# Taylor-attention sandwich, 1 core: the rest features in tiles of 64 rows and 32 columns, split over two PSUM banks

## The chip, the core and the metric

One core of one Trainium2 chip. The metric is the device time of one execution in microseconds (us), as the median of several runs. TensorE (PE), VectorE (DVE), ScalarE (ACT) and GpSimd (POOL) each work off a queue of their own, in order, and wait for each other on semaphores; the DMA queues are fed by SyncE (SP) and by ACT.

## What is computed

The input is 16 sequences of 512 rows of 256 numbers, float32. Cut to what matters:

```python
x = x + layernorm(attention(layernorm(x)))
x = x + layernorm(ffn(layernorm(x)))

# attention: 16 heads of 16, rotary q and k, no softmax but its Taylor form
t = 1.0 + qk + 0.5 * qk * qk
attn = t / jnp.sum(t, axis=-1, keepdims=True)
wv = einsum('bhkq,bhqd->bhkd', attn, v);  return wv @ w_o

# ffn: rows and weights rounded to an FP6 grid in blocks of 32, then one product
out = xd @ wd.T + bias
```

Because 1 + s + s*s/2 is a polynomial in products of q and k, the kernel never forms the 512 x 512 scores. It expands each head's key into features (products of pairs of its 16 numbers, squares, the numbers themselves, a one), sums features times values over the 512 rows of a sequence, and multiplies the features of the other side with these sums.

## The kernel before

The work is cut into 64 tiles of 128 rows, four to a sequence. Every engine's program is a loop over steps, `step(n)`, in which each stage is called for the tile `n` minus its lag. The table `LAG` gives the lags, `FIRST` and `FINAL` shift the first 12 and the last 16 tiles, and the order of calls inside `step` is the order on that engine (PE at lines 822 to 846). So an engine's order is written out by hand and nothing is scheduled at run time: an engine that waits holds up all that stands behind it.

One tile passes PE in these stages, here with their lines:

- `turn_z` (672): two 128x128 transposes into `ps_tr`. ACT reads them into `hT` (991), splits off the high part `hT_h` (1001), POOL the low part `hT_l` (1472).
- `project_kq` (591, 592, 594): six products of 512 columns into `ps_qk`; DVE reads that bank twice for the rotation (1270, 1278). `project_v`: six of 256 columns into `ps_tr`.
- `turn_q` (658): four transposes into `ps_tr`, read by ACT (1022). The bank `ps_tr` has four users a tile, `turn_z`, `turn_q`, `project_v`, `turn_ffn_input`, and each waits until the one before was read.
- `sum_features` (796): 16 products of 32 output rows and 161 columns into `ps_mt`, four at a time side by side in the array (tiles of 128 rows and 32 columns).
- `select_0` to `select_4` (635): each one product of 512 columns with a 0/1 matrix from the constant `selection`. ACT squares each result into a slice of `feat` (944, 946). The first four slices are one head each with 128 features; the fifth, `feat[:, p2, HQ]`, holds for four heads together the remaining 32 features of each, in rows 32h to 32h+31.
- `attend` (687, 690): for each of four heads 32 output rows and 512 columns in `ps_o`. The first product takes the head's 128 features with weights `main`. The second takes the fifth slice with weights `rm`, a 128x128 block of which only the 32x32 block of the own head is not zero. ACT copies the result into `osb` with a bias (1032), `copy_quad`.
- `turn_quads` (724) and `turn_attention` (715) in `ps_o`; `project_out` in `ps_w`; `turn_ffn_input` in `ps_tr`; `ffn` (767, 591, 592, 594) in `ps_w` too, except for the last eight tiles, where it is in `ps_qk`.

After `ffn` comes one chain across four engines: ACT sums squares (`square_f`, 1067), POOL adds a floor and takes the power -1/2 (1488, 1492), DVE scales and adds (`add_ffn`, 1388), SP stores. `project_out` has the same chain (1048, 1488, 1492, 1355).

Once a sequence, after its fourth tile, ACT copies the sums (956), PE turns them (`turn_sums`, 805), ACT copies `main` (966), PE forms the matrix of the rest (`rest_matrix`, 814, 818) and ACT copies it to `rm` (`copy_rest`, 973, four instructions).

## Time and profile before

| | us |
|---|---|
| median of 3 runs | 675.56 (674.57 to 675.61) |
| the profiled execution | 673.7 |
| its span | 671.8 |
| PE busy | 660.0, 98% |
| ACT busy | 558.0, 83% |
| DVE busy | 562.8, 84% |
| POOL busy | 335.2, 50% |

The span runs from the first to the last instruction of the profiled execution; 1.9 us lie around it. PE instructions are pipelined and the ends of their rows are modelled, so they overlap: how long a group really holds PE is read from the start of one row to the start of the next. In the middle of the kernel every tile is alike, so one tile's rows stand for all.

### The profile page before, as it was taken

What the parts mean: (1) busy time and instruction counts of PE and PEld (TensorE: products, weight loads), DVE (VectorE), ACT (ScalarE), POOL (GpSimd) and SP (SyncE); (2) the same over time, 40 slices, a digit from 0 to 9 for tenths busy, and PEclk for the clock granted to TensorE, in tenths of its full rate; (3) what the DMA queues carried; (4) which work ended last, traced back from release to release, by engine and by line L of the source; (5) the groups of instructions that cost most, each with busy time, mean ns of one, the idle gap of its engine ahead of it and who ended that gap; (6) DMA issues with size and microseconds to landing.
All of it is one profiled execution on the core that took longest, in us unless ns stands there. A gap on an engine that the chain in (4) does not pass through costs nothing.

```text
span 671.8 us, 20456 instructions
## 1 busy us (share of the span) xinstructions
PE 660.0 (98%) x6772; PEld 505.7 (75%) x6772; DVE 562.8 (84%) x1460; ACT 558.0 (83%) x1551; POOL 335.2 (50%) x723
## 2 busy tenths in 40 slices
PE   7889999999999999999999999999999999999998
PEld 6766677777777777877777787777778777777578
DVE  5998889888988888898888889888888988986675
ACT  4578999798898979888897988889798888989864
POOL 3654435545554554555455455545544554643354
PEclk8999999999999999999999999999999999999999
DMA  7101100202011010201101020111102001010101
GB/s 236 33 3 32 34 1 3 80 17 81 9 49 48 30 60 18 79 11 48 50 32 58 17 81 9 49 48 37 55 17 80 11 18 49 9 50 23 51 33 40
DMA packets 28165, 28.35 MB, mean 42 GB/s; under 512 B 1824, under 2 KB 27936, under 8 KB 28064
## 3 DMA queue, kind: packets, MB, share of 16 engines
q1 hardware_dynamic: 27248, 26.26, 12.2%
q8 instruction: 58, 0.95, 0.6%
q10 hardware_dynamic: 816, 0.79, 0.4%
q14 instruction: 43, 0.35, 0.2%
HBM read 18.65 MB, written 8.39 MB: 40 GB/s over the span
## 4 chain that ended last, share of the span: by engine, by line
PE 94%; DVE 2%; ACT 2%; issue 1%; POOL 1%; DVEq 0%; POOLq 0%; ACTq 0%
PE ps_f L635 11%; PE ps_mt L796 10%; PE ps_o L687 9%; PE ps_o L690 8%; PE ps_qk L591 5%; PE ps_qk L594 5%; PE ps_qk L592 4%; PE ps_w L591 4%; PE ps_w L592 4%; PE ps_w L594 4%; PE ps_tr L658 4%; PE ps_tr L591 4%; PE ps_o L724 4%; PE ps_tr L594 2%; PE ps_tr L592 2%; PE ps_tr L672 2%
## 5 line engine op out<-in xcount | busy, mean ns | idle before, releaser
L944 ACT ACTIVATE feat<-ps_f 128x512 f32<-128x512 f32 x256 | 153.1, 601 | 1.8 <-PE ps_f L635 1.1
L635 PE MATMUL ps_f<-qT,selr 128*128 128x512 f32 x320 | 136.1, 428 | 0.7 <-ACT feat L944 0.5
L527 DVE TENSOR_TENSOR kf<-kf 128x1024 f32<-128x1024 f32 (+1 forms) x128 | 135.7, 1095 | 0.2
L1488 POOL TENSOR_TENSOR ve_y<-var_y,epst 128x1 f32<-128x1 f32 x64 | 24.4, 382 | 167.0 <-ACT squares_y L1048 167.0
L796 PEld LDWEIGHTS ps_mt<-kf,vp 128*32 128x32 f32 x2048 | 65.5, 110 | 38.6 <-issue 35.5
L796 PE MATMUL ps_mt<-kf,vp 128*32 128x161 f32 x2048 | 82.2, 301 | 0.1
L991 ACT ACTIVATE hT<-ps_tr,small,lnwx 128x128 f32<-128x128 f32 x128 | 51.6, 454 | 24.5 <-PE ps_tr L672 23.7
L687 PE MATMUL ps_o<-feat,main 128*32 128x512 f32 x512 | 68.2, 603 | 0.0
L690 PE MATMUL ps_o<-feat,rm 128*32 128x512 f32 x512 | 67.0, 592 | 0.0
L635 PEld LDWEIGHTS ps_f<-qT,selr 128*128 128x128 f32 x320 | 60.3, 189 | 8.7 <-issue 4.7
L1488 POOL TENSOR_TENSOR ve_f<-var_f,epst 128x1 f32<-128x1 f32 x64 | 14.5, 227 | 103.6 <-ACT squares_f L1067 103.6
L1007 ACT ACTIVATE vp<-ps_tr 128x256 f32<-128x256 f32 x64 | 24.6, 384 | 46.2 <-PE ps_tr L594 44.3
L527 POOL TENSOR_TENSOR kf<-kf 128x256 f32<-128x256 f32 x64 | 49.0, 765 | 18.3 <-DVE kf L1294 18.3
L1472 POOL TENSOR_TENSOR hT_l<-hT,hT_h 128x256 fp32r<-128x256 f32 x64 | 47.1, 736 | 18.6 <-ACT hT_h L1001 18.6
L591 PE MATMUL ps_qk<-wkqv_h,hT_l 128*128 128x512 f32 x128 | 51.3, 401 | 0.0
L1477 POOL TENSOR_TENSOR qsp<-kf,qsp 128x256 fp32r<-128x256 f32 x64 | 47.0, 735 | 8.2 <-ACT qsp L1038 5.2
L592 PE MATMUL ps_qk<-wkqv_l,hT_h 128*128 128x512 f32 x128 | 50.7, 396 | 0.0
L1032 ACT ACTIVATE osb<-ps_o,cb 128x512 f32<-128x512 f32 x64 | 44.9, 701 | 2.3 <-PE ps_o L690 2.2
L946 ACT ACTIVATE feat<-ps_f,small 128x512 f32<-128x512 f32 x64 | 46.0, 719 | 0.7 <-PE ps_f L635 0.3
L1287 DVE TENSOR_TENSOR kf<-t 128x512 f32<-128x512 f32 x64 | 44.5, 696 | 1.6
L690 PEld LDWEIGHTS ps_o<-feat,rm 128*32 128x32 f32 x512 | 17.4, 110 | 37.5 <-issue 37.5
L1388 DVE SCALAR_TENSOR_TENSOR fin<-ps_w,rs_f,xs 128x256 f32<-128x256 f32 x56 | 27.0, 482 | 22.1 <-POOL rs_f L1492 22.1
(194 smaller groups left out, 1989.9 us busy)
## 6 DMA issues: line engine op xcount, KB each, us to landing
xc<-L_attn_x SPq DMA_DIRECT2D x16, 512.0 KB, 4.0
result<-fin SPq DMA_DIRECT2D x64, 128.0 KB, 1.7
xa<-L_attn_x SPq DMA_DIRECT2D x15, 512.0 KB, 4.0
wkqv<-L_attn_w_kv ACTq DMA_DIRECT2D x2, 256.0 KB, 4.8
xa<-L_attn_x SPq DMA_DIRECT2D x1, 384.0 KB, 6.3
csel<-selection SPq DMA_DIRECT2D x1, 320.0 KB, 6.7
wkqv<-L_attn_w_q ACTq DMA_DIRECT2D x1, 256.0 KB, 4.4
wf<-L_ffn_weight SPq DMA_DIRECT2D x1, 256.0 KB, 6.1
```

Of the source, the lines that this page charges most:

```text
L527: return eng.tensor_tensor(dims(row, F_MAIN, [[FW, heads], [HD, NR], [1, HD]]), dims(row, F_LIN, [[FW, heads], [0, NR], [1, HD]]), dims(ro ...
L591: pe.matmul(out_, xl(c), wh(c), start=c == 0 and not bias, stop=False)
L592: pe.matmul(out_, xh(c), wl(c), start=False, stop=False)
L594: mm = pe.matmul(out_, xh(c), wh(c), start=False, stop=c == CH - 1)
L635: pe.matmul(ps_f[i % 2][:, :], selr[:, i], qT[:, par, quad], start=True, stop=True).then_inc(sel_done, 1)
L687: pe.matmul(ps_o[VW * h:VW * (h + 1), :], main[:, par, quad, VW * h:VW * (h + 1)], feat[:, p2, h], start=True, stop=False, skip_group_chec ...
L690: mm = pe.matmul(ps_o[VW * h:VW * (h + 1), :], rm[:, par, quad, VW * h:VW * (h + 1)], feat[:, p2, HQ], start=False, stop=True, skip_group_ ...
L796: mm = pe.matmul(ps_mt[qd // 2][VW * h:VW * (h + 1), (qd % 2) * NF:(qd % 2 + 1) * NF], vp[:, s2, qd * HQ + h], kf[:, s2, qd * HQ + h, 0:NF ...
L944: act.activation(feat[:, p2, i], ps_f[i % 2][:, :], ACT.Square).then_inc(squared, 1)
L991: ins = act.activation(hT[:, c], ps_tr[:, c * P:(c + 1) * P], ACT.Identity, bias=lnb[:, c:c + 1], scale=lnwx[:, c:c + 1])
L1472: pool.tensor_tensor(hT_l[:, p2], hT[:], hT_h[:, p2].bitcast(F32), ALU.subtract).then_inc(hT_low, 1)
L1477: pool.tensor_tensor(dims(qsp[:, p2], HQ * HD, [[2 * HQ * HD, NQ], [HD, HQ], [1, HD]]), dims(kf[:, p2, 0, 0:1], F_Q, [[HQ * FW, NQ], [FW, ...
```

## The change

- The fifth slice. Its 32 features a head are in 32 of 128 rows, so 64 rows hold two heads. `select_4` becomes two products of 256 columns: the first 256 columns with the selection as before, the last 256 with a second selection matrix in which the heads are moved by two places (rows of heads 0, 1 and of heads 2, 3 change places).
- `attend` writes columns 0 to 255 to `ps_o` and columns 256 to 511 to `ps_w` (`quad_bank`). The products with `main` become eight of 256 columns in place of four of 512. The products with the rest become eight of 64 rows and 32 columns, 256 columns long. For heads 0 and 1 the first part takes array rows 0 to 63 and the second part rows 64 to 127, for heads 2 and 3 the other way round.
- The second part needs the rest weights in the other half of the rows: `copy_rest` on ACT waits for its own copy and issues two DMAs from `rm` to a second buffer `rm_moved`, once a sequence.
- `copy_quad` becomes two ACT instructions of 256 columns.
- `ps_w` now holds half of `attend`, so `ffn` goes to `ps_qk` for all tiles. `project_kq` now waits for `fin_ready`, the end of the chain behind `ffn`; `ffn` waits for both readings of keys and queries; `attend` waits for `xs_ready`, and `project_out` for `o_copied`.
- The selection constant grows from five to six blocks and is loaded into `osb` (alias `csel`).
- The tables `LAG`, `FIRST`, `FINAL` and the order of calls in every `step` are new.

```diff
-    "fill_a": 0, "warm_up": -19, "turn_ffn_input": 15, "rest_matrix": 4, "fill_b": 2, "drain_a": 16, "attend": 8,
+    "warm_up": -20, "drain_b": 16, "turn_z": 0, "rest_matrix": 3, "project_kq": 1, "select_0": 7,
...
+                sel[:, h, i, HQ + 1, ((h + 2) % HQ * 2 + kind) * HD + i] = 1.0
...
+        quad_bank = [ps_o, ps_w]
...
-                pe.matmul(ps_f[i % 2][:, :], selr[:, i], qT[:, par, quad], start=True, stop=True).then_inc(sel_done, 1)
+                if i < HQ:
+                    pe.matmul(ps_f[i % 2][:, :], selr[:, i], qT[:, par, quad], start=True, stop=True).then_inc(sel_done, 1)
+                else:
+                    for part in range(2):
+                        mm = pe.matmul(ps_f[0][:, part * TH:(part + 1) * TH], selr[:, HQ + part], qT[:, par, quad, part * TH:(part + 1) * TH],
+                                       start=True, stop=True)
+                    mm.then_inc(sel_done, 1)
...
+                wait(pe, xs_ready, issued["project_out"])
+                wait(pe, wdt_copied, CH * issued["turn_ffn_weight"])
                 pe.wait_ge(rm_copied, t.seq + 1)
+                pe.wait_ge(rest_moved, 32 * (t.seq + 1))
                 pe.wait_ge(squared, CHUNKS * (n + 1))
-                for h in range(HQ):
-                    pe.matmul(ps_o[VW * h:VW * (h + 1), :], main[:, par, quad, VW * h:VW * (h + 1)], feat[:, p2, h],
-                              start=True, stop=False, skip_group_check=True)
-                for h in range(HQ):
-                    mm = pe.matmul(ps_o[VW * h:VW * (h + 1), :], rm[:, par, quad, VW * h:VW * (h + 1)], feat[:, p2, HQ],
-                                   start=False, stop=True, skip_group_check=True)
+                for part in range(2):
+                    for h in range(HQ):
+                        pe.matmul(quad_bank[part][VW * h:VW * (h + 1), 0:TH], main[:, par, quad, VW * h:VW * (h + 1)],
+                                  feat[:, p2, h, part * TH:(part + 1) * TH], start=True, stop=False, skip_group_check=True)
+                for part in range(2):
+                    for h in range(HQ):
+                        half = (h // 2 + part) % 2
+                        rows = slice(64 * half, 64 * half + 64)
+                        weights = (rm, rm_moved)[part]
+                        mm = pe.matmul(quad_bank[part][VW * h:VW * (h + 1), 0:TH], weights[rows, par, quad, VW * h:VW * (h + 1)],
+                                       feat[rows, p2, HQ, part * TH:(part + 1) * TH], start=False, stop=True, skip_group_check=True)
...
             def project_kq(t):
...
                 wait(pe, qk_read, 2 * (t.n - 1))
+                wait(pe, fin_ready, issued["ffn"])
...
             def ffn(t):
...
+                wait(pe, qk_read, 2 * issued["project_kq"])
+                wait(pe, fin_ready, issued["ffn"])
...
             def copy_rest(t):
...
                 ins.then_inc(rm_copied, 1)
+                act.wait_ge(rm_copied, t.seq + 1)
+                for half in range(2):
+                    act.dma_start(rm_moved[64 * half:64 * half + 64, mpar], rm[64 - 64 * half:128 - 64 * half, mpar]).then_inc(rest_moved, 16)
...
             def copy_quad(t):
...
-                act.activation(osb[:, par, quad], ps_o[:, :], ACT.Identity, bias=cb[:, par, quad:quad + 1]).then_inc(o_copied, 1)
+                for part in range(2):
+                    ins = act.activation(osb[:, par, quad, part * TH:(part + 1) * TH], quad_bank[part][:, 0:TH], ACT.Identity,
+                                         bias=cb[:, par, quad:quad + 1])
+                ins.then_inc(o_copied, 1)
...
```

Where the rows move. First PE around `attend`, in a tile in the middle, before (a name in brackets is a semaphore that the instruction waits for, x3 a count):

```order
L645 MATMUL ps_tr<-small,xd 128x128
L687 MATMUL ps_o<-feat,main 32x512 [waits rm_copied,aT_low,squared,norm_ready,o_copied]
L687 MATMUL ps_o<-feat,main 32x512 x3
L690 MATMUL ps_o<-feat,rm 32x512 x4
L796 MATMUL ps_mt0<-kf,vp 32x161 [waits sq_ready,feat_ready2,v_copied,feat_ready1,feat_ready0]
L796 MATMUL ps_mt0<-kf,vp 32x161 x7
L796 MATMUL ps_mt1<-kf,vp 32x161 x8
L591 MATMUL ps_tr<-wkqv_h,hT_l 128x256 [waits xdT_low,qT_copied,v_copied,hT_copied,hT_low]
```

And the same place on PE after the change:

```order
L618 MATMUL ps_f1<-qT,selr 128x512 [waits squared]
L790 MATMUL ps_mt0<-kf,vp 32x161 [waits sq_ready,feat_ready2,v_copied,feat_ready1,feat_ready0]
L790 MATMUL ps_mt0<-kf,vp 32x161 x7
L790 MATMUL ps_mt1<-kf,vp 32x161 x8
L680 MATMUL ps_o<-feat,main 32x256 [waits wdt_copied,rm_copied,xs_ready,rest_moved,aT_low,squared,norm_ready,o_copied]
L680 MATMUL ps_o<-feat,main 32x256 x3
L680 MATMUL ps_w<-feat,main 32x256 x4
L688 MATMUL ps_o<-feat,rm 32x256 x4
L688 MATMUL ps_w<-feat,rm_moved 32x256 x4
L572 MATMUL ps_tr<-wkqv_h,hT_l 128x256 [waits xdT_low,qT_copied,v_copied,hT_copied,hT_low]
```

`sum_features` has moved ahead of `attend`, and between the 32-column products of 128 rows and the full-width products of `project_v` there are now products of 64 rows.

Second, PE around `project_kq` before, behind the last selection of a tile (`ps_f`):

```order
L635 MATMUL ps_f0<-qT,selr 128x512 [waits squared]
L591 MATMUL ps_qk<-wkqv_h,hT_l 128x512 [waits qk_read,hT_low]
L592 MATMUL ps_qk<-wkqv_l,hT_h 128x512
L591 MATMUL ps_qk<-wkqv_h,hT_l 128x512
L592 MATMUL ps_qk<-wkqv_l,hT_h 128x512
L594 MATMUL ps_qk<-wkqv_h,hT_h 128x512 x2
L724 MATMUL ps_o<-small,osb 128x128 [waits norm_ready,aT_low,o_copied]
L724 MATMUL ps_o<-small,osb 128x128 x3
L672 MATMUL ps_tr<-small,z 128x128 [waits xdT_low,qT_copied,v_copied,hT_copied,z_ready]
L672 MATMUL ps_tr<-small,z 128x128
```

And after:

```order
L622 MATMUL ps_f0<-qT,selr 128x256 [waits squared]
L622 MATMUL ps_f0<-qT,selr 128x256
L722 MATMUL ps_o<-small,osb 128x128 [waits norm_ready,aT_low,o_copied]
L722 MATMUL ps_o<-small,osb 128x128 x3
L661 MATMUL ps_tr<-small,z 128x128 [waits xdT_low,qT_copied,v_copied,hT_copied,z_ready]
L661 MATMUL ps_tr<-small,z 128x128
L572 MATMUL ps_qk<-wkqv_h,hT_l 128x512 [waits fin_ready,qk_read,hT_low]
L573 MATMUL ps_qk<-wkqv_l,hT_h 128x512
L572 MATMUL ps_qk<-wkqv_h,hT_l 128x512
L573 MATMUL ps_qk<-wkqv_l,hT_h 128x512
L575 MATMUL ps_qk<-wkqv_h,hT_h 128x512 x2
```

`project_kq` has moved behind `turn_quads` and `turn_z` and waits for `fin_ready`. From the end of `ffn` to it PE now passes `turn_attention`, `select_3`, `turn_q`, `project_out`, the two halves of `select_4`, `turn_quads` and `turn_z`.

Third, ACT once a sequence, where it copies the rest matrix, before:

```order
L991 ACTIVATE hT<-ps_tr,small,lnwx 128x128 [waits hT_low,zT_done]
L991 ACTIVATE hT<-ps_tr,small,lnwx 128x128
L944 ACTIVATE feat<-ps_f0 128x512 [waits quad_done,sel_done]
L1061 ACTIVATE squares_s,var_s<-c3 128x256 [waits rstd_s,centred]
L1048 ACTIVATE squares_y,var_y<-ps_w 128x256 [waits rstd_y,wo_done]
L1014 ACTIVATE xdT_h<-ps_tr 128x256 [waits ffn_done,xdT_done]
L1001 ACTIVATE hT_h<-hT 128x256 [waits v_done,qk_done,hT_copied]
L973 ACTIVATE rm<-ps_mt0 32x4x32 [waits ps_done]
L973 ACTIVATE rm<-ps_mt0 32x4x32 x3
```

And after:

```order
L1043 ACTIVATE kf<-kf 128x16x16 [waits rope_ready]
L988 ACTIVATE hT<-ps_tr,small,lnwx 128x128 [waits hT_low,zT_done]
L988 ACTIVATE hT<-ps_tr,small,lnwx 128x128
L967 ACTIVATE rm<-ps_mt0 32x4x32 [waits ps_done]
L967 ACTIVATE rm<-ps_mt0 32x4x32 x3
L971 DMA rm_moved<-rm 64x512 [waits rm_copied]
L971 DMA rm_moved<-rm 64x512
L998 ACTIVATE hT_h<-hT 128x256 [waits v_done,qk_done,hT_copied]
L1061 ACTIVATE squares_s,var_s<-c3 128x256 [waits rstd_s,centred]
```

The copy of the rest matrix, with a wait for its own end and two DMA issues behind it, now stands ahead of `hT_h` and of all that follows in that step.

## Rows read from the trace of the kernel before

**Rows 1.** The page: span, busy time, chain by engine, DVE's products of features.
```profile
span 671.8 us, 20456 instructions
PE 660.0 (98%) x6772; PEld 505.7 (75%) x6772; DVE 562.8 (84%) x1460; ACT 558.0 (83%) x1551; POOL 335.2 (50%) x723
...
PE 94%; DVE 2%; ACT 2%; issue 1%; POOL 1%; DVEq 0%; POOLq 0%; ACTq 0%
...
L527 DVE TENSOR_TENSOR kf<-kf 128x1024 f32<-128x1024 f32 (+1 forms) x128 | 135.7, 1095 | 0.2
```

**Rows 2.** Busy time by stretch: us, each engine, PE clock, DMA share, GB/s.
```profile
400.00:500.00 100.00, 100.00 (x1027) 77.26 (x1027) 84.64 (x225) 86.42 (x243) 51.43 (x113) 1.00 0.12 38
640.00:671.80 31.80, 29.81 (x234) 26.04 (x234) 21.75 (x72) 16.49 (x61) 15.48 (x42) 1.00 0.12 38
```

**Rows 3.** Timeline of PE: start, length, engine, line, tiles, form, count.
```profile
305.95 0.48 PE L818 MATMUL ps_mt<-small,rest 128*32 128x32 f32 x32
306.38 1.06 PE L687 MATMUL ps_o<-feat,main 128*32 128x512 f32 x8
...
313.77 0.60 PE L724 MATMUL ps_o<-small,osb 128*128 128x128 f32 x4
314.21 0.38 PE L672 MATMUL ps_tr<-small,z 128*128 128x128 f32 x2
...
315.61 0.38 PE L645 MATMUL ps_tr<-small,xd 128*128 128x128 f32 x2
315.92 1.06 PE L687 MATMUL ps_o<-feat,main 128*32 128x512 f32 x8
316.81 1.04 PE L690 MATMUL ps_o<-feat,rm 128*32 128x512 f32 x8
317.67 1.28 PE L796 MATMUL ps_mt<-kf,vp 128*32 128x161 f32 x32
318.87 0.39 PE L591 MATMUL ps_tr<-wkqv_h,hT_l 128*128 128x256 f32 x1
319.10 0.28 PE L592 MATMUL ps_tr<-wkqv_l,hT_h 128*128 128x256 f32 x1
319.22 0.28 PE L591 MATMUL ps_tr<-wkqv_h,hT_l 128*128 128x256 f32 x1
...
325.41 1.06 PE L687 MATMUL ps_o<-feat,main 128*32 128x512 f32 x8
...
345.53 1.06 PE L687 MATMUL ps_o<-feat,main 128*32 128x512 f32 x7
```

**Rows 4.** Timeline of PE and its weight loads (PEld) inside one `attend`.
```profile
306.81 0.15 PEld L690 LDWEIGHTS ps_o<-feat,rm 128*32 128x32 f32 x4 [0.27 <-issue]
307.24 1.07 PE L690 MATMUL ps_o<-feat,rm 128*32 128x512 f32 x8
```

**Rows 5.** Timeline of all engines, the chain behind one `ffn`, in order.
```profile
311.46 0.39 PE L635 MATMUL ps_f<-qT,selr 128*128 128x512 f32 x1
...
311.81 0.39 ACT L1067 ACTIVATE squares_f<-ps_w 128x256 f32<-128x256 f32 x1
...
312.37 0.20 POOL L1488 TENSOR_TENSOR ve_f<-var_f,epst 128x1 f32<-128x1 f32 x1 [2.24 <-ACT squares_f L1067]
...
312.65 0.55 POOL L1492 TENSOR_TENSOR rs_f<-ve_f,mhalf 128x1 f32<-128x1 f32 x1
...
313.23 0.48 DVE L1388 SCALAR_TENSOR_TENSOR fin<-ps_w,rs_f,xs 128x256 f32<-128x256 f32 x1 [0.39 <-POOL rs_f L1492]
```

**Rows 6.** Timeline of ACT in one tile: its copies and its idle time.
```profile
327.42 0.71 ACT L1032 ACTIVATE osb<-ps_o,cb 128x512 f32<-128x512 f32 x1
329.38 0.38 ACT L1007 ACTIVATE vp<-ps_tr 128x256 f32<-128x256 f32 x1 [1.25 <-PE ps_tr L594]
...
333.61 0.81 ACT L991 ACTIVATE hT<-ps_tr,small,lnwx 128x128 f32<-128x128 f32 x2 [0.45 <-PE ps_tr L672]
```

**Rows 7.** Timeline of ACT: four copies to `rm`; a DMA issue near the start.
```profile
306.91 1.09 ACT L973 ACTIVATE rm<-ps_mt 32x128 f32<-32x128 f32 x4
...
1.21 0.49 ACTq L855 DMA_DIRECT2D wkqv<-L_attn_w_q  x1
```

436 lines of the change are left out of this document (206 added, 230 removed).

## The prediction

> **What bounds the kernel now.** The page first: PE is busy for 98% of the span and holds 94% of the chain that ended last [rows 1]. In the middle of the kernel PE is busy all the time, at its full clock, while ACT and DVE are busy for 86% and 85% [rows 2]. A busy PE may still be a slow one, since the ends of its rows are modelled, so I went to its timeline and read starts. One `attend` begins at 315.92 and the next at 325.41: 9.49 us a tile. From there to 345.53 are two tiles, 20.12 us, so the one in which `turn_sums` and `rest_matrix` come in takes 20.12 - 9.49 = 10.63; four tiles take 345.53 - 306.38 = 39.15 us [rows 3]. In these starts no product waits for a semaphore: a product of 256 columns holds PE for 0.12 us (319.10 to 319.22), a transpose for 0.11 (313.77 to 314.21 for four), and the rows follow each other at these distances. So a microsecond less of PE work in a tile is a microsecond less of time, as long as no wait steps into its place. ACT sat idle for 1.25 us before one read of `project_v` and 0.45 before the next `hT` [rows 6]; that is the room in which ACT may grow.
>
> **The products with the rest.** Now they run from 316.81 to 317.67, 0.86 us, for two passes of 512 columns with four heads side by side; one pass of 512 columns is 0.43 [rows 3]. After the change eight products of 256 columns stand in eight tiles of the array (two of rows, four of columns). If all eight run at once, two passes of 256 columns take 2 x 0.215 = 0.43. That removes 0.43 us a tile, 64 x 0.43 = 27.5 us. Eight starts must fit into 0.215 us; the 32 products of 32 columns at 305.95 are through in 0.43 us, 13 ns each [rows 3], so eight need 0.11 and issue doesn't bind.
>
> **The products with `main`.** Four passes of 256 columns in place of two of 512. A fixed cost per pass would show in `sum_features`: its 8 rounds of 161 columns would take 8 x 0.43 x 161/512 = 1.08 us by columns alone, and take 1.20 with the change of form behind them (317.67 to 318.87) [rows 3]. I take 0, and 0.05 at most.
>
> **One more change of form.** Going from full-width products into the 32-column form costs little: 315.61 to 315.92 is 0.31 for two transposes worth 0.22, so 0.09. Coming out costs 1.20 - 1.08 = 0.12 in front of `project_v` and another 0.11 on its first product, which holds PE for 0.23 in place of 0.12: 0.23 in all [rows 3]. `attend` keeps one entry and one exit, since `sum_features` only changes sides with it, and gets one more change between 128 rows and 64 rows. No row shows that one. Its bounds are 0 and 0.23; I take 0.12, near the entry, because the products behind it have the same short weight loads as those behind the entry. That is 64 x 0.12 = +7.7 us (0 to 14.7). The Trainium skill, TensorEngine Tiling (Array Packing), section Key Properties, says that changing the tiling mode drains TensorE while using another tile of the same mode doesn't; by it the term is there, and without it the sum would be 7.7 us lower. The 0.09 and 0.23 of the trace agree with a drain; no run here shows one between 128 and 64 rows.
>
> **`select_4` in two halves.** Twice 256 columns at 0.12 against one product of 512 at about 0.23 to 0.24: +0.01 a tile, +0.6 us (0 to 1.3).
>
> **`copy_quad` in two.** One copy of 512 columns lasts 0.71, one of 256 columns from PSUM 0.38 [rows 6]: at most 0.05 us more, on ACT, covered by the 1.25 us idle. On the path: 0. If that cover were gone it would be 3 us.
>
> **Once a sequence on ACT.** The wait for its own copy (about 0.1) and two DMA issues: the issue at 1.21 holds ACT's queue for 0.49 [rows 7], so 2 x 0.49 + 0.1 = 1.1 us. And the four copies to `rm`, 1.09 us [rows 7], which stood behind `hT_h`, now stand ahead of it, of `squares_s`, of the first square and of the copy of the feed-forward input. So in that step all of them are 2.2 us later; PE's own step is longer by `rest_matrix`, about 0.7 of the 1.14 us by which the long tile exceeds the plain one, and ACT's idle time gives 1.25. That leaves 0.2 of 2.2 to show. The copies to `rm` also release `sum_features`, which stands about 2 us behind `rest_matrix` (`project_kq` of 1.4, two selections and two transposes); they end 1.1 us plus their wait behind it, in time. So 16 x 0.2 = +3.2 us; bounds 0 and, with all of the 1.1 new microseconds showing, 17.6. The landing of `rm_moved` isn't on the path: `attend` for the new sequence comes two steps behind the copy, about 19 us.
>
> **The bank of keys and queries.** This is the new wait that could take the gain. `ffn` and `project_kq` now share `ps_qk`. Behind `ffn`: the next PE product starts at 311.46, the square at 311.81, POOL's two at 312.37 and 312.65, `fin` at 313.23 and it ends at 313.71 [rows 5], 2.25 us after 311.46. In the new order PE has in that time `turn_attention` 0.22, `select_3` 0.24, `turn_q` 0.24 to 0.44, `project_out` 6 x 0.12 = 0.72, `select_4` 0.24, `turn_quads` 0.44, `turn_z` 0.22: 2.3 to 2.5 us. The margin is 0.1 to 0.25 us, enough if ACT, POOL and DVE are at hand as they were here (POOL waited 2.24 for the square, `fin` 0.39 for POOL). Behind `wait(pe, fin_ready)` stands all of PE. On the other side, from `project_kq` to `ffn`, PE has about 4.3 us of other work and DVE two reads of about 0.7 us each: room. The bank `ps_w` goes the opposite way: `attend` must find it read by `add_attention`. I take 0 for both.
>
> **The ends.** From 640 us on PE is bound by the chain from one `ffn` to the next, busy for 29.8 of 31.8 us, much of it with idle products [rows 2]; `ffn` was already in `ps_qk` there. Nothing is gained, and the new tables may move it by 2 us either way.
>
> **The sum**: -27.5 + 7.7 + 0.6 + 3.2 = -16.0 us. Against the profiled execution, 673.7 with its span of 671.8 and 1.9 around it, that is 657.7. That execution is 1.9 us below the median of 675.6, so the median after should be about 659.6. In the trace a plain tile should take 9.49 - 0.43 + 0.12 + 0.01 = 9.19 us.
>
> **Rivals.**
>
> *`fin` comes late, slower.* DVE works in order, and its products of features last 1.095 us each in the mean [rows 1]. `add_ffn` stands between two of them. If DVE is in the middle of one when POOL is done, `fin` is 0.55 us later; less the margin of 0.2, PE waits 0.35 us a tile at `project_kq`, more than the 0.30 gained: 0.05 x 64 + 3.2 = +6, 682. It decides from a delay of about 0.5 us. For it: three engines are now 90% busy (8.1 to 8.3 of 9.19 us) and have less slack. Against: ahead of `fin` stands a wait for ACT's `attT_h`, so DVE is there and idle. 7 in 100.
>
> *The eight tiles don't run side by side.* The trace shows four column tiles at once, never two row tiles. If the second part waits for the first, the rest takes 4 x 0.215 = 0.86 as before and the costs stay: +7.7 + 0.6 + 3.2, 687. The two parts use different row halves for the same columns and write different banks, which speaks against it. 6 in 100.
>
> *The weight loads show.* In [rows 4] the loads for the rest start at 306.81, 0.43 before its products at 307.24, beneath the products with `main` in the same rows: hidden. If they were hidden only in part with short passes, two more rounds of loads of 0.11 would add up to 0.22 a tile, 14 us: 674, no change. The Trainium skill, TensorE: Matmul & The Clock Gate, section Packing small matmuls, says that a load overlaps running products only where the row group differs; by that rule the loads would show, and this trace disagrees with it. 4 in 100.
>
> *Partly filled.* PE waits in places for ACT or DVE: the copies that free `ps_tr`, the step of the rest matrix with its full 1.1 us (+14 us), the exit price for the added change (+7). One of them gives 667 to 674. 18 in 100.
>
> **Numbers.** The forecast, 652 to 667, holds 63 in 100; 2 more lie below it, where the added change costs nothing and ACT hides all (-26.9, 649). With the rivals that makes faster 0.81, same 0.06, slower 0.13; 0.2%, 1.35 us, is about what a measurement can tell from no change. The range 651 to 672 takes in the bounds of the added change and most of those of ACT's step.
>
> **What would show it.** Right: starts of `attend` 9.2 us apart in plain tiles; the products with `rm` and `rm_moved` (line 688) through in about 0.45 us; `project_kq` directly behind `turn_z`. Wrong: the last four products at line 688 starting 0.4 us behind the first four; a gap ahead of `project_kq` with `fin` at its end; a gap ahead of `turn_ffn_input` or `project_v` in the tile of `rest_matrix`; DVE or ACT without idle time. The forecast fails if three engines at 90% can't keep a PE that never waits.

## The result: 1.25% slower

| | before | after |
|---|---|---|
| median of the runs | 675.1 us (674.3 to 675.6) | 683.0 us (681.9 to 685.8) |
| ratio to before | | 1.0125 (95%: 1.0091 to 1.0158) |
| span of the profiled execution | 671.8 us | 680.0 us |
| plain tile, `attend` to `attend` | 9.49 us | 9.36 us |
| four tiles in the middle of the kernel | 39.15 us | 39.12 us |
| last `attend` to last `fin` | 27.6 us | 31.7 us |

The forecast was 659.6 us with a range of 651 to 672: 23 us too fast, and outside the range. The page of after, span, busy time, chain by engine, and the row of the new DMAs, which are issued on ACT's queue (16 sequences, two each):

```profile
span 680.0 us, 22840 instructions
...
PE 656.5 (97%) x7856; PEld 518.5 (76%) x7856; DVE 561.9 (83%) x1460; ACT 575.9 (85%) x1615; POOL 389.5 (57%) x723
...
PE 73%; ACT 10%; issue 7%; DVE 3%; POOL 3%; ACTq 2%; DMA 1%; POOLq 0%; DVEq 0%
...
rm_moved<-rm ACTq DMA_DIRECT2D x32, 128.0 KB, 2.7
```

Beside [rows 1]: PE is busy for 3.5 us less and idle for 23.5 us where it was 11.8. The chain holds PE for 73%, not 94%, and ACT, its queue and "issue" have come in. By stretch (as [rows 2], us and busy time of PE, PEld, DVE, ACT, POOL, then clock, DMA share, GB/s):

```profile
400.00:500.00 100.00, 99.49 (x1238) 79.23 (x1240) 84.54 (x229) 89.52 (x253) 61.91 (x113) 1.00 0.17 47
640.00:680.00 40.00, 36.12 (x319) 31.17 (x310) 28.98 (x95) 23.87 (x82) 20.53 (x52) 1.00 0.11 38
```

PE now has half a microsecond idle in 100 us in which it had none, and 3.9 us from 640 us on, which was 2.0. PE's timeline around one `attend`, which answers to [rows 3]:

```profile
332.59 1.30 PE L790 MATMUL ps_mt<-kf,vp 128*32 128x161 f32 x32
333.81 0.64 PE L680 MATMUL ps_o<-feat,main 128*32 128x256 f32 x8
334.24 0.64 PE L680 MATMUL ps_w<-feat,main 128*32 128x256 f32 x8
334.81 0.42 PE L688 MATMUL ps_o<-feat,rm 64*32 64x256 f32 x4
334.84 0.42 PE L688 MATMUL ps_w<-feat,rm_moved 64*32 64x256 f32 x4
335.05 0.40 PE L688 MATMUL ps_o<-feat,rm 64*32 64x256 f32 x4
335.08 0.40 PE L688 MATMUL ps_w<-feat,rm_moved 64*32 64x256 f32 x4
335.40 0.39 PE L572 MATMUL ps_tr<-wkqv_h,hT_l 128*128 128x256 f32 x1
```

The tiling does what it says: `ps_o` and `ps_w` start 0.03 us apart, so eight tiles run side by side, and the next pass is 0.24 behind. The rest took 0.86 us in before; two passes at 0.24 are 0.48. The change into the 64-row form takes 0.12 to 0.14 of that back (the last pass with `main`, worth 0.43 by columns, lasts until 334.81, 0.57 us). The way out of the column form is paid in both kernels: here it is in the 0.59 from 334.81 to 335.40, in before it stands behind `sum_features`. So the tiling should save 0.24 to 0.26 us a tile, but the tile is only 0.13 shorter. Where PE waits (line, busy, mean ns, idle time before the group and what ended it):

```profile
L572 PE MATMUL ps_tr<-wkqv_h,hT_l 128*128 128x256 f32 x128 | 39.2, 328 | 7.0 <-POOL hT_l L1472 3.5 <-DVE xdT_l L1344 3.3
...
L761 PE MATMUL ps_qk<-bias,ones 128*128 128x256 f32 x64 | 19.0, 296 | 2.5 <-DVE fin L1388 2.3
```

`project_v` waits 7.0 us, which is 1.9 in before. What it waits for comes from POOL and DVE, the low parts `hT_l` and `xdT_l`, and both are made from the high parts that ACT writes. `ffn` waits 2.5 us, 2.3 of it for `fin`, all of it after 640 us. And ACT's timeline in the step of the rest matrix:

```profile
341.86 0.83 ACT L967 ACTIVATE rm<-ps_mt 32x128 f32<-32x128 f32 x3
342.72 1.12 ACTq L971 DMA_DIRECT2D rm_moved<-rm  x2
343.96 0.42 ACT L998 ACTIVATE hT_h<-hT 128x256 fp32r<-128x256 f32 x1 [1.27 <-issue]
```

The two issues hold ACT's queue for 1.12 us and ACT stands still for 1.27. My theory from the two traces (A): the tiling gains 0.26 us a tile, and three things take it back: the issues on ACT, something between `sum_features` and `attend`, and the new order with the feed-forward product in the bank of keys and queries. The rivals: the tiling itself doesn't pay in this kernel (B), or the issues on ACT are nearly the whole (C).

### The profile page after: what moved, and what is told of

Its sections match the earlier page's. It is cut to its first block, busy times and chain, and to the rows that moved or that the text cites. A ratio compares the mean times of both kernels' runs of the same rounds, so it can differ in the third digit from the quotient of the medians.

```text
span 680.0 us, 22840 instructions
## 1 busy us (share of the span) xinstructions
PE 656.5 (97%) x7856; PEld 518.5 (76%) x7856; DVE 561.9 (83%) x1460; ACT 575.9 (85%) x1615; POOL 389.5 (57%) x723
## 4 chain that ended last, share of the span: by engine, by line
PE 73%; ACT 10%; issue 7%; DVE 3%; POOL 3%; ACTq 2%; DMA 1%; POOLq 0%; DVEq 0%
PE ps_mt L790 9%; PE ps_f L618 7%; PE ps_qk L572 5%; PE ps_qk L575 5%; PE ps_qk L573 5%; PE ps_o L680 4%; PE ps_o L688 4%; PE ps_tr L572 4%; PE ps_w L680 3%; PE ps_o L722 3%; PE ps_tr L647 3%; PE ps_w L572 2%; PE ps_tr L575 2%; PE ps_tr L573 2%; ACTq L971 2%
## 5 line engine op out<-in xcount | busy, mean ns | idle before, releaser
L512 DVE TENSOR_TENSOR kf<-kf 128x768 f32<-128x768 f32 (+1 forms) x128 | 144.5, 1131 | 0.2
L618 PE MATMUL ps_f<-qT,selr 128*128 128x512 f32 x256 | 110.0, 439 | 0.5 <-ACT feat L938 0.2
L1488 POOL TENSOR_TENSOR ve_y<-var_y,epst 128x1 f32<-128x1 f32 x64 | 48.5, 758 | 41.2 <-ACT squares_y L1048 41.2
L1270 DVE TENSOR_TENSOR t<-ps_qk,cosT 128x512 f32<-128x512 f32 x64 | 44.1, 689 | 32.1 <-PE ps_qk L575 31.9
L1492 POOL TENSOR_TENSOR rs_x<-ve_x,mhalf 128x1 f32<-128x1 f32 x64 | 56.5, 883 | 4.7
L1030 ACT ACTIVATE osb<-ps_o,cb 128x256 f32<-128x256 f32 x64 | 30.5, 477 | 23.2 <-PE ps_w L688 22.1
L1337 DVE TENSOR_TENSOR attT_l<-ps_o,attT_h 128x256 fp32r<-128x256 f32 x56 | 23.8, 424 | 31.4 <-ACT attT_h L977 30.2
L572 PEld LDWEIGHTS ps_tr<-wkqv_h,hT_l 128*128 128x128 f32 x128 | 24.0, 187 | 31.3 <-issue 17.5
L572 PE MATMUL ps_tr<-wkqv_h,hT_l 128*128 128x256 f32 x128 | 39.2, 328 | 7.0 <-POOL hT_l L1472 3.5
L1388 DVE SCALAR_TENSOR_TENSOR fin<-ps_qk,rs_f,xs 128x256 f32<-128x256 f32 x64 | 30.9, 482 | 17.1 <-POOL rs_f L1492 16.9
```

The source lines that it names most:

```text
L512: return eng.tensor_tensor(dims(row, F_MAIN, [[FW, heads], [HD, NR], [1, HD]]), dims(row, F_LIN, [[FW, heads], [0, NR], [1, HD]]), dims(ro ...
L572: pe.matmul(out_, xl(c), wh(c), start=c == 0 and not bias, stop=False)
L618: pe.matmul(ps_f[i % 2][:, :], selr[:, i], qT[:, par, quad], start=True, stop=True).then_inc(sel_done, 1)
L1488: pool.tensor_tensor(ve[c][:, t.two:t.two + 1], variance, floor, ALU.add).then_inc(pool_step[c], 1)
L1492: pool.tensor_tensor(rs[c][:, t.two:t.two + 1], ve[c][:, t.two:t.two + 1], mhalf[:], ALU.pow).then_inc(rstd[c], 1)
```

## The experiments

Each is given with its edit, what was expected, and what was measured. The times by trace are starts of `attend`; "four tiles" is the distance from `attend` 21 to `attend` 49, over 7.

| run | us | ratio to before (95%) | plain tile | four tiles |
|---|---|---|---|---|
| after | 683.0 | 1.0125 (1.0091 to 1.0158) | 9.36 | 39.12 |
| e1 SyncE issues the copies | 673.4 | 0.9981 (0.9972 to 0.9991) | 9.37 | 38.80 |
| e2 six waits ahead of `sum_features` | 706.5 | 1.0473 (1.0441 to 1.0504) | 9.84 | 40.73 |
| e3 no row tiling | 680.2 | 1.0085 (1.0070 to 1.0100) | 9.51 | 39.32 |
| e4 tiling in the kernel before | 726.3 | 1.0764 (1.0746 to 1.0782) | 10.09 | 41.06 |
| e5 e1, `attend` with two waits | 666.3 | 0.9879 (0.9865 to 0.9894) | 9.23 | 38.24 |
| e6 e5, fewer waits on `ps_tr` too | 665.7 | 0.9870 (0.9855 to 0.9885) | 9.23 | 38.19 |
| e7 before, fewer waits on `ps_tr` | 674.0 | 0.9992 (0.9982 to 1.0002) | 9.49 | 39.16 |
| e8 e6, two banks for `ffn` at the end | 663.6 | 0.9834 (0.9818 to 0.9850) | 9.23 | 38.22 |
| e9 e3 with three idle waits | 680.4 | 1.0087 (1.0070 to 1.0103) | 9.50 | 39.31 |
| e10 before with three idle waits | 679.5 | 1.0073 (1.0058 to 1.0089) | 9.56 | 39.54 |
| e11 after, `attend` with two waits | 679.0 | 1.0060 (1.0037 to 1.0083) | 9.22 | 38.73 |
| e12 e1, the wait for `xs` last | 665.6 | 0.9872 (0.9856 to 0.9888) | 9.23 | 38.21 |
| e13 e3, two banks for `ffn` at the end | 678.2 | 1.0053 (1.0038 to 1.0068) | 9.50 | 39.31 |
| e14 before, rest matrix moved | 680.6 | 1.0095 (1.0080 to 1.0110) | 9.49 | 39.57 |
| e15 after with three edits | 663.9 | 0.9833 (0.9813 to 0.9853) | 9.23 | 38.23 |

### Who issues the copies (e1)

```
 # ScalarE, copy_rest
-                act.wait_ge(rm_copied, t.seq + 1)
-                for half in range(2):
-                    act.dma_start(rm_moved[...], rm[...]).then_inc(rest_moved, 16)
 # SyncE, first in its step
+            def move_rest(t):
+                sp.wait_ge(rm_copied, t.seq + 1)
+                for half in range(2):
+                    sp.dma_start(rm_moved[...], rm[...]).then_inc(rest_moved, 16)
+                once(n, "copy_rest", move_rest)
```

> The changed kernel with one edit: the two transfers that make the second copy of the rest weights are issued by SyncE instead of ScalarE. Theory A (the tiling gains 0.26 us a tile on TensorE, and three smaller things take it back: the two issues on ScalarE, waits that attend can only issue once sum_features has drained, and a longer pipe with the feed-forward in the bank of keys and queries): in the trace of after the step that follows the rest matrix costs 0.41 us more than in before, of which the issues (1.12 us between copy_rest and hT_h) are the whole, so 16 x 0.4 = 6.4 us go, 676.6 us, range 675 to 679. Rival C (the issues on ScalarE are the main loser, at the start of the program too, where they stand ahead of hT_h): more than 10 us go, under 673. If the step is late for another reason, the time stays at 683.

Measured: 673.4 us, 9.6 less, between A and C. ACT in the same step, the last three copies to `rm` and the next row:

```profile
336.17 0.83 ACT L973 ACTIVATE rm<-ps_mt 32x128 f32<-32x128 f32 x3
337.03 0.42 ACT L1001 ACTIVATE hT_h<-hT 128x256 fp32r<-128x256 f32 x1
```

`hT_h` starts 0.86 us behind the start of the copies' row in place of 2.10, and `project_v` waits 1.3 us in the whole kernel, not 7.0. Four tiles are 0.32 shorter. By the two traces 9.1 us are gained: 6.2 from the first `attend` to the last, and 2.9 before the first (57.4 for 60.3). A's 6.4 had only the first part.

Only one pair of issues stands ahead of the first `attend`, so the 2.9 are more than its own length. After, one pair and what follows on PE, then PE, PEld, DVE, ACT, POOL and the granted clock from 40 to 60 us:

```profile
45.77 1.22 ACTq L971 DMA_DIRECT2D rm_moved<-rm  x2
48.85 0.38 PE L572 MATMUL ps_tr<-wkqv_h,hT_l 128*128 128x256 f32 x1 [1.46 <-POOL hT_l L1472]
50.38 1.09 PE L647 MATMUL ps_tr<-identr,qsp 128*128 128x128 f32 x4 [0.56 <-ACT vp L1004]
40.00:50.00 10.00, 7.95 (x120) 5.88 (x112) 8.41 (x20) 6.89 (x19) 5.40 (x9) 1.00 0.28 80
50.00:60.00 10.00, 9.42 (x68) 7.42 (x69) 8.49 (x15) 7.03 (x18) 7.07 (x7) 0.83 0.01 3
```

The same in e1:

```profile
48.99 0.63 PE L653 MATMUL ps_tr<-identr,qsp 128*128 128x128 f32 x4 [0.56 <-ACT vp L1007]
40.00:50.00 10.00, 9.02 (x131) 6.96 (x124) 9.55 (x22) 7.62 (x22) 6.17 (x10) 1.00 0.27 59
50.00:60.00 10.00, 9.78 (x124) 6.91 (x126) 9.90 (x17) 8.57 (x21) 7.18 (x9) 1.00 0.07 24
```

`turn_q` is 1.4 us late (50.38 for 48.99): that is the issues. The other 1.5 come behind it, where the granted clock of TensorE is at the lower of its two levels for a part of the stretch (0.83 in the mean, 1.00 in e1), after a stretch in which PE was busy for 7.95 us of 10 and not 9.02. The six products of `project_kq` take 2.5 us there and 1.4 in e1. The runs agree in size: e11 below took 676.8 us in its one run at full clock and 679.0 to 680.0 in the three whose mean clock was 0.995. So about 1.5 of the 9.6 us is the price of the clock, which followed from the issues in this trace.

### Without the row tiling (e3)

```
 # attend: 128 rows, all 512 elements, one bank
-                for part in range(2): ... quad_bank[part] ... (rm, rm_moved)[part] ...
+                for h in range(HQ):
+                    pe.matmul(ps_o[VW * h:VW * (h + 1), :], main[...], feat[:, p2, h], start=True, stop=False)
+                for h in range(HQ):
+                    mm = pe.matmul(ps_o[VW * h:VW * (h + 1), :], rm[...], feat[:, p2, HQ], start=False, stop=True)
 # select_4 one product, copy_quad one copy, no rm_moved; attend doesn't wait for xs,
 # project_out not for o_copied
```

> The changed kernel without the row tiling: the rest products are again 128 rows by 32 columns over all 512 elements into one bank, the selection is one product, copy_quad one copy, and there is no second copy of the weights; the new order of the stages and the feed-forward in the bank of keys and queries stay. Theory A: the tile pays 0.265 us more for the rest products (64 x 0.265 = +17.0), and saves the issues on ScalarE (-6.4) and some of attend's waits (0 to -3.4): 690 to 694 us. Rival B (the tiling gives nothing that the kernel keeps, its price is the form change and the waits): 683 or less. If it comes out near 675, order and bank cost nothing and the tiling is the loss.

Measured: 680.2 us. That is 2.8 less than after, but 6.8 more than e1, which differs from it by the tiling and what comes with it, three waits of `attend` among it. So B falls: with its copies on SyncE the tiling pays, though 6.8 and not 17. And the new order and the feed-forward's bank cost 0.85% against before, without any tiling. PE's timeline around `attend`:

```profile
330.85 1.30 PE L773 MATMUL ps_mt<-kf,vp 128*32 128x161 f32 x32
331.97 1.04 PE L669 MATMUL ps_o<-feat,main 128*32 128x512 f32 x8
332.83 1.04 PE L672 MATMUL ps_o<-feat,rm 128*32 128x512 f32 x8
333.80 0.39 PE L572 MATMUL ps_tr<-wkqv_h,hT_l 128*128 128x256 f32 x1
```

From `sum_features` to `attend` are 1.12 us; in after 1.22. The 0.1 is idle time that the tiled kernel alone has.

### The waits of `attend` (e2, e5, e11)

In after `attend` has eight waits on PE, in the untiled kernel five. e2 issued six of them ahead of `sum_features`:

```
+                attend_waits(...)      # o_copied, norm_ready, aT_low, wdt_copied, rm_copied, rest_moved
                 each(n, "sum_features", sum_features)
                 each(n, "attend", attend)   # waits for xs_ready and squared only
```

> The changed kernel with one edit: six of attend's eight waits on TensorE are issued ahead of sum_features; only the waits for xs and for the squares stay where attend begins. Theory A: between the last sum_features product and the first attend product lie 0.106 us in which two stand-alone waits are issued although what they wait for is done, so 64 x 0.106 = 6.8 us go at most and, if one of the two records stays, half of it: 676 to 680 us. Rival D (the 0.106 us is the change of tile form, or the arrival of xs): no change, 683 us.

Measured: 706.5 us, 23.5 more: a miss for both sides. The row of `sum_features`, which had 1.3 us of idle time before it:

```profile
L794 PE MATMUL ps_mt<-kf,vp 128*32 128x161 f32 x2048 | 83.3, 302 | 32.1 <-DVE att L1336 20.2 <-issue 9.9 <-ACT wdt L918 1.3
```

The wait for `norm_ready` is for `att`: `sum_features` waits 20.2 us for it. In after DVE starts it at 332.71 and `sum_features` starts at 332.59: it is done in time for `attend`, and moved ahead its wait holds `sum_features`. The run says nothing of the 0.1 us. e5 leaves waits out instead, those that follow from the two that stay:

```
                 # attend, tiles 9 to 56, on top of e1
-                wait(pe, o_copied, ...)  wait(pe, norm_ready, ...)  wait(pe, aT_low, ...)
                 wait(pe, xs_ready, issued["project_out"])
-                wait(pe, wdt_copied, ...)  pe.wait_ge(rm_copied, t.seq + 1)
+                if t.tile == 0:
                     pe.wait_ge(rest_moved, 32 * (t.seq + 1))
                 pe.wait_ge(squared, CHUNKS * (n + 1))
```

> The first experiment's kernel (SyncE issues the copy of the weights) with attend's waits cut from eight to the two that the others follow from (xs and the squares; the wait for the copied weights stays for the first tile of a sequence) for tiles 9 to 56; the first and last eight keep them. Theory A: the kernel of the first experiment has 0.11 us more between the last sum_features product and the first attend product than the untiled kernel, with two stand-alone waits in it, and they go: 48 x 0.11 = 5.3 us of 673.4, so 668 us (667 to 670). Rival D (the gap is the tile form or the bank of the second half): 673.4.

The waits for the copied feed-forward weights and for `rm` are left out behind the fill, that for `rest_moved` in all but the first tile of a sequence. Measured: 666.3 us, 7.1 less than e1, and the plain tile is 9.23. The gap is in the waits, not in the tile form. The same cut in after, with ACT still issuing the copies (e11):

> The changed kernel with attend's waits cut to two and nothing else: ScalarE still issues the copies of the weights. If the pieces add: 683.0 - 7.1 (what the cut gave behind SyncE's issues) = 676, so still no faster than before. If ScalarE's step comes to matter more once TensorE is faster: up to 678.

Measured: 679.0 us, 4.0 less than after and not 7.1. Plain tiles are 9.22, but the tile behind the rest matrix is 9.64 to 10.02, and `project_v` waits 10.0 us in all in place of 7.0: with a faster PE the 1.1 us on ACT show more. The two causes don't simply add.

### Fewer waits elsewhere (e6, e7)

```
 # turn_z, turn_q, turn_ffn_input, project_v
-                wait(pe, hT_copied, issued["turn_z"])
-                wait(pe, qT_copied, issued["turn_q"])
-                wait(pe, xdT_low, issued["turn_ffn_input"])
-                wait(pe, v_copied, issued["project_v"])
+                turned_bank_is_free()      # waits for the last user of ps_tr alone
```

> As the kernel with attend's two waits, and each of the four users of the bank of transposes waits for the user before it alone instead of for all four. Theory A: behind attend stand the five waits of project_v, 0.12 us apart, the last 0.1 us before its first load; its first product comes 0.11 us after the rest products end. If that 0.11 is the waits, 64 x 0.1 = 6 us more go, 662 us; if it is the end of the 32-column form (0.09 us in the untiled kernel too), nothing more, 668. Range 660 to 669.

> The kernel before with the same cut in the waits of the four users of the bank of transposes, nothing else. It tells whether the cost of issuing waits behind a full queue was there before: its project_v stands behind 32 products of sum_features and has five waits, three of them in the last 0.4 us. If they cost, 64 x 0.1 to 0.2 = 6 to 12 us go, 663 to 669 us; if they are hidden, 674.7.

Measured: 665.7 us, 0.6 less than e5, and 674.0, 0.6 less than before with an interval that takes in no change. So waits as such cost about nothing in these places. The 0.11 us in front of `project_v` stay, which leaves the way out of the column form for them. What made those of `attend` cost?

### Number, place or the late one (e9, e10, e12)

e9 adds three waits that have long been passed to the untiled kernel, eight in all:

```
                 wait(pe, aT_low, ...)
+                wait(pe, hT_low, issued["project_kq"])
+                wait(pe, wdt_copied, CH * issued["turn_ffn_weight"])
                 pe.wait_ge(rm_copied, t.seq + 1)
+                pe.wait_ge(mt_copied, t.seq + 1)
                 pe.wait_ge(squared, CHUNKS * (n + 1))
```

> The untiled kernel with three more waits ahead of attend, on semaphores that have long been passed (hT_low, the copied weights of the feed-forward, mt_copied), so eight as in after. Theory A (issuing the waits costs, whatever they wait for): in the untiled kernel the first attend product follows the last sum_features product by 0.117 us, in the tiled one with eight waits by 0.224, with two by 0.117; here 0.224 again, 64 x 0.11 = +7 us on 680.2, 686 to 688. Rival (only a wait whose releaser is late costs, here xs): 680.2.

Measured: 680.4 us, 0.2 more. My theory A, that issuing the waits costs whatever they wait for, is refuted in this place, and the rival holds. The wait instructions themselves are in the trace, on the queue of the weight loads. In the packed trace each record names the semaphores that it waits for, two at most: the eight waits of `attend` are four records, and the eighth semaphore is on the first weight load. A record shows the line of one of its waits only. Of e9, the records with `rm_copied` and with `mt_copied` (duration in ns, lowest/median/highest, of the 26 between 250 and 500 us; start of the first and the last):

```profile
L668 PEldq EVENT_SEMAPHORE  x26: 51/51/51, 253.1 to 499.8; - x26
...
L669 PEldq EVENT_SEMAPHORE  x26: 51/51/51, 253.2 to 499.9; - x26
```

Of e1, the last three of the four, in the order in which they stand ahead of `attend`:

```profile
L681 PEldq EVENT_SEMAPHORE  x26: 497/528/534, 249.7 to 493.2; - x26
...
L682 PEldq EVENT_SEMAPHORE  x26: 51/51/51, 250.3 to 493.8; - x26
...
L683 PEldq EVENT_SEMAPHORE  x26: 51/51/51, 250.4 to 493.9; - x26
```

One of e1's lasts 0.53 us in every tile. It carries line 681, the wait for `rm_copied`, which was passed long before, and it has a second semaphore, the one that DVE raises behind `xs`. In one tile it runs from 327.27 to 327.80, and this is DVE there:

```profile
327.27 0.48 DVE L1358 SCALAR_TENSOR_TENSOR xs<-ps_w,rs_y,xc 128x256 f32<-128x256 f32 x1
```

It ends 0.05 us after `xs`; so it is `xs` that it waits for. Behind it the two other records follow at 327.86 (`rest_moved` and `aT_low`) and 327.99 (`squared` and `norm_ready`), the first load of `attend` at 328.07 and the product at 328.10; the last of the 32 products of `sum_features` started at 327.85, and in the untiled kernel `attend` follows that one by 0.12. Had nothing stood between `xs` at 327.75 and the load, the load would have been in time. That is theory F: a wait that is passed costs nothing while the engine has work queued, but those that stand behind a late one, here two records 0.13 apart, put off the load. e12 changes the order alone:

```
                 wait(pe, aT_low, min(issued["turn_attention"], TILES - NT * 2))
-                wait(pe, xs_ready, issued["project_out"])
                 wait(pe, wdt_copied, CH * issued["turn_ffn_weight"])
                 pe.wait_ge(rm_copied, t.seq + 1)
                 pe.wait_ge(rest_moved, 32 * (t.seq + 1))
                 pe.wait_ge(squared, CHUNKS * (n + 1))
+                wait(pe, xs_ready, issued["project_out"])
```

> The first experiment's kernel (SyncE issues the copy of the weights) with all eight waits of attend, only their order changed: the wait for xs, fourth of eight, becomes the last. Theory F (formed after the run with three idle waits: a wait that is passed costs nothing while the engine has queued work, but xs comes 0.2 us before the last sum_features product ends, and two waits at 0.13 us and a load stand behind it): the gap between sum_features and attend falls from 0.224 to 0.117 us, as with two waits: 673.4 - 7 = 666.5 us. Rival (it is the number of waits, or one of those cut): 673.4.

Measured: 665.6 us, 7.8 less than e1, from one line that moved. PE's timeline, and one of its waits at `attend`, at 51 ns like the two ahead of it. The semaphore of `xs` is now in the last record ahead of the load, on the line of a helper (321), at 335.19:

```profile
334.24 1.30 PE L796 MATMUL ps_mt<-kf,vp 128*32 128x161 f32 x32
335.35 0.61 PE L686 MATMUL ps_o<-feat,main 128*32 128x256 f32 x8
...
336.33 0.42 PE L694 MATMUL ps_o<-feat,rm 64*32 64x256 f32 x4
...
336.92 0.39 PE L578 MATMUL ps_tr<-wkqv_h,hT_l 128*128 128x256 f32 x1
```

```profile
L682 PEldq EVENT_SEMAPHORE  x26: 51/51/51, 258.4 to 496.9; - x26
```

From `sum_features` to `attend` are 1.11 us again, as in the untiled kernel, with the same number of records as in e1. F is borne out. e10 asks the same of before, where `attend` stands behind two transposes:

```
                 wait(pe, aT_low, ...)
+                wait(pe, hT_low, issued["project_kq"])
+                wait(pe, v_copied, issued["project_v"])
                 pe.wait_ge(rm_copied, t.seq + 1)
+                pe.wait_ge(mt_copied, t.seq + 1)
                 pe.wait_ge(squared, CHUNKS * (n + 1))
```

> The kernel before with three more waits ahead of attend that have long been passed (hT_low, v_copied, mt_copied). There attend stands behind two transposes and not behind 32 products of sum_features. In the trace the last of its wait records on TensorE's sequencer is over 0.21 us before its first load. Theory A by that slack: three records at 0.11 us, 0.12 us exposed, 64 x 0.12 = +8 us, 682; if the sequencer runs ahead far enough there, nothing: 674.6. Range 674 to 683: it tells whether the place or the number decides.

Measured: 679.5 us, 5.0 more. Four tiles take 0.39 more, 0.10 a tile: behind a short queue waits cost even where all are passed. The three waits are two more records, all of 51 ns. So the place decides first, and the order of the waits second.

### The tiling in the kernel before (e4)

```
+        quad_bank = [ps_o, ps_qk]       # attend's second half in the bank of keys and queries
 # lags, orders and ffn_bank of before; SyncE issues the copies; DVE's step:
                 each(n, "extend_k", extend_k)
+                each(n, "products_0", products, 0)
                 each(n, "add_ffn", add_ffn)
+                each(n, "rope_cos", rope_cos)
+                each(n, "rope_sin", rope_sin)
```

> The kernel before (its order of stages on TensorE, ScalarE and GpSimd, its lags and its banks for the feed-forward) with the row tiling alone: the second half of attend goes into the bank of keys and queries, which stands free between the two rope reads and the next projection; for that VectorE reads that bank earlier in its step (rope_cos and rope_sin behind add_ffn, the first products ahead of it). SyncE issues the copy of the weights. Theory A: the order and the feed-forward's move are what costs, so here the tiling's gain is kept: 675.1 - 64 x 0.265 = 658 us, range 655 to 668 (one step of VectorE may come late). Rival B (the tiling itself doesn't pay): 675 or more. Rival E (the reads of keys and queries come late for attend, about 0.5 us a tile): 685 to 700, with attend's waits for t (rope) in the trace.

Measured: 726.3 us, a miss beyond every range:

```profile
L710 PE MATMUL ps_o<-feat,main 128*32 128x256 f32 x512 | 41.8, 395 | 28.3 <-DVE att L1363 16.5 <-issue 9.8 <-DVE t L1311 1.0
```

Not the reads of keys and queries (`t`, 1.0 us) came late, as rival E had it, but `att`, which my order of DVE had put behind them: it holds the bank of `attend`. The rest products themselves are nearly as in after (396 and 397 ns in the mean, 388 in after). The run prices a bad order of DVE, not the tiling. Whether before's order can take the tiling with a second bank stays open; another order of DVE wasn't tried.

### The ends and the order (e8, e13, e14)

e8 and e13 let the feed-forward products behind the last `attend` alternate between two banks, in the tiled kernel (on top of e6) and in the untiled one (on top of e3):

```
+        def ffn_bank(t):
+            return ps_o if t.n in after_attend and t.n % 2 else ps_qk
 # ffn behind the last attend
+                    wait(pe, fin_ready, t.n - 2)      # was: issued["ffn"]
```

> As the kernel with all those waits cut, and the feed-forward products that come after the last attend alternate between the bank of keys and queries and the bank of attend, which is free by then. Theory A (the shared bank makes the end longer): in the trace of after the feed-forward products wait 2.3 us for fin in that bank, four times, all at the end, so 2 to 3 us less than the kernel with the waits cut alone. Rival (the end is bounded by the chain over ScalarE, GpSimd and VectorE that makes fin, whatever the bank): within 0.5 us of it.

> The untiled kernel with the feed-forward products after the last attend alternating between two banks. If the feed-forward's single bank is what makes the end of the new order longer, as in the tiled kernel (2.1 us), 680.2 - 2.1 = 678.1 us; if the end is bound elsewhere without the tiling, 680.2.

Measured: 663.6 and 678.2 us, 2.1 and 2.0 less. The 2.5 us of idle time of `ffn` in `ps_qk` are gone in e13:

```profile
L756 PE MATMUL ps_qk<-bias,ones 128*128 128x256 f32 x60 | 17.4, 290 | 0.1
L756 PE MATMUL ps_o<-bias,ones 128*128 128x256 f32 x4 | 1.2, 307 | 0.5 <-DVE xdT_l L1332 0.5
```

Two of the 5.7 us that the untiled kernel is behind before are that. Another part is in the middle: its four tiles take 39.32 and not 39.15, and all of it is in the tile of the rest matrix (10.81 for 10.63). There `rest_matrix`, in 32-column form, stands between `turn_z` and `project_kq`; in before it stood ahead of `attend`, which needs that form anyway. e14 moves it so in before:

```
-    "rest_matrix": 4,
+    "rest_matrix": 3,
 # PE's step
-                once(n, "rest_matrix", rest_matrix)      # between turn_ffn_input and attend
                 each(n, "turn_z", turn_z)
+                once(n, "rest_matrix", rest_matrix)
```

> The kernel before with the step of the rest matrix moved on TensorE from between turn_ffn_input and attend to behind turn_z of the step before, where its neighbours are no products of 32 columns. In the traces the rest matrix costs 0.154 us of gaps in before (it enters the 32-column form that attend needs anyway) and 0.30 in the untiled kernel (in and out again). Theory: 16 x 0.15 = +2.4 us, 677.0; the rival that the earlier rest matrix frees something that sum_features waits for: 674.6 or a little less.

Measured: 680.6 us, 6.1 more and not 2.4. The tile with the rest matrix is 10.80 for 10.63, the 0.17 expected, the same as in the untiled kernel. The other 0.25 a sequence is in the tile behind it (9.80 for 9.55), where `sum_features` now waits for the copies to `rm`; that part is e14's own, and the untiled kernel hasn't it (9.52).

### The three edits together (e15)

```
 after + the copies issued by SyncE (e1) + the wait for xs last (e12) + two banks for ffn at the end (e8)
```

> The changed kernel with three edits: SyncE issues the copies of the weights, attend's wait for xs is the last of its eight, and the feed-forward products after the last attend alternate between two banks. If the causes add: 683.0 - 9.6 - 7.9 - 2.1 = 663.4 us, range 662.5 to 664.5. If the cut in the waits of the other stages, which the fastest kernel so far has besides, is needed: 664 to 665.

Measured: 663.9 us, in the range, and 1.67% faster than before (1.47 to 1.87). It matches e8, 663.6, which has fewer waits besides. From the page of e15, span, busy time and chain:

```profile
span 662.3 us, 22848 instructions
...
PE 646.8 (98%) x7856; PEld 516.3 (78%) x7856; DVE 560.2 (85%) x1460; ACT 579.4 (87%) x1615; POOL 387.5 (59%) x723
...
PE 90%; DVE 3%; ACT 2%; issue 2%; DMA 1%; POOL 1%; ACTq 0%; DVEq 0%; POOLq 0%
```

## Why the prediction was wrong

The way from before to after in four steps, each the difference of two runs (ratios to before, times 675):

| step | runs | predicted | measured |
|---|---|---|---|
| order, lags, feed-forward in `ps_qk` | before to e3 | 0, within 2 | +5.7 |
| row tiling: rest products, form, two selections, two copies | e3 to e12 | -19.2 | -14.4 |
| the wait for `xs` in `attend` | e12 to e1 | 0 | +7.4 |
| ACT's step once a sequence | e1 to after | +3.2 (0 to 17.6) | +9.7 |
| sum | | -16.0 | +8.4 |

The last two rows depend on the order in which the steps are taken. From e5 over e11 to after, ACT's step is +12.2 and the waits of `attend` +4.4; their sum is the same within 1 us.

Against the forecast the four rows miss by 5.7, 4.8, 7.4 and 6.5 us, 24.4 in all. So no single step explains the result: three costs were set to nothing or nearly so, and the gain was taken too large.

**What bounds the kernel: right, and not enough.** PE at every start was the right bound; that "no product waits for a semaphore" was read as room, but it held for the old order of waits and stages.

**The products with the rest and the change of form: right, a little too good.** Eight tiles run side by side, so the rival of 6 in 100 fell. A pass costs 0.24 and not 0.215; `main` to rest is 336.33 - 335.35 = 0.98 in e12 and 0.86 in e3, so the change into 64 rows costs 0.12, the value taken. The Trainium skill, TensorEngine Tiling (Array Packing), section Key Properties, says that a change of the tiling mode drains TensorE; the trace agrees, and 0.12 us is what it comes to here. The plain tile fell by 0.28 from e3 to e12, where 0.30 were predicted. Times 64 that is 17.8 us, and 14.4 came: from the first `attend` to the 49th the tiling saves 12.0 us (461.0 to 449.0), in the last 15 tiles 2.0 (124.1 to 122.2) and from the last `attend` to the last `fin` nothing (31.9 and 31.8); 0.4 are ahead of the first. So the factor of 64 was mis-sized. The weight loads didn't show, and that rival fell.

**The bank `ps_w`: the step that failed outright.** "`attend` must find it read by `add_attention`. I take 0": it finds it read 0.2 us before it needs it, but with two wait records behind. The prediction counted what is waited for and not what stands in the same row of waits. 7.4 us.

**ACT's step: the mechanism right, the size wrong.** 0.2 us was to show of 2.2. In the middle 0.08 a tile shows, 0.32 a sequence; from the first `attend` to the last that comes to 6.2 us. Another 2.9 come before the first `attend`, 1.4 from one pair of issues and 1.5 at the lower clock, and the sum had neither. The issue was put at 0.49 and is 0.56; the 0.1 for ACT's wait for its own copy had no row, and ACT stands still for 0.15 longer than the issues last (1.27 and 1.12). The size is within the bounds of 0 to 17.6, and the rival of waits that come in part (18 in 100) had named this step at +14.

**The bank of keys and queries: right in the middle, wrong at the end.** `project_kq` never waits for `fin` in steady state, so the rival of 7 in 100 fell: the mechanism it named didn't act. But behind the last `attend` the feed-forward waits 2.5 us for its own bank, worth 2.0 (e13). The prediction had said that `ffn` "was already in `ps_qk` there", which was true of before too, where it waits 0.4; in the new order nine feed-forward products are left when the last `attend` begins, where there were eight.

**The order: taken at 0.** It costs 0.17 us a sequence for one more way in and out of the 32-column form (2.7 us). Of 5.7 us, 2.0 and 2.7 are so accounted for; about 1 is left, in the fill and the end, and wasn't separated. The order of before and after was at hand, and `rest_matrix` between two 128-column stages could be seen in it.

**The chances.** Slower had 0.13. No rival that ends on the slower side was the one that came; what came was the sum of three losses of 6 to 10 us, each of which the text had named as a place and set to nothing or nearly so.

## What to carry to other kernels

Put the wait that comes late last, next to the instruction that needs it: passed waits are free while the engine has work queued, and cost about 0.1 us a record behind a late one or a short queue. See in the trace where the late one ended up, since the records aren't in the order of the source. Don't issue DMAs from an engine that is nine tenths busy when SyncE can do it. A gain per tile is worth its number of tiles only where that engine bounds the time, and several places set to 0 in a sum need one range for their sum.

## What the runs showed of the hardware

- Passes of eight tiles of 64 rows and 32 columns into two banks, 256 columns each, follow each other at 0.24 us (0.215 by columns). The way into that form from 128 rows costs 0.12.
- A passed wait on TensorE takes 51 ns in its record and the next record comes 0.11 to 0.14 later. Two more records behind 32 queued products cost nothing (e9), behind two transposes 0.10 a tile (e10); two behind a late one cost 0.11 and more (e12 against e1).
- One record can hold two waits and shows the line of only one (e1, line 681): it is the time at which it ends that tells what it waited for.
- In the fill of after the granted clock was 0.83 from 50 to 60 us, behind a stretch with PE busy for 7.95 us of 10; in e1, with 9.02, it stayed at 1.00. It cost about 1.5 us.
- Two DMA issues hold ScalarE's queue for 1.12 us, and ScalarE idles for 1.27 around them.
